# Sums of the resident weights made in DRAM by accumulating transfers instead of in pieces on GpSimd

## What is computed

```python
x = x + tanh(g_xattn[0]) * xattn(layernorm(x), ctx, mask, q_w, k_w, v_w, o_w, q_norm_w, k_norm_w)
x = x + tanh(g_ffn[0]) * ffn(layernorm(x), A, B, Wr)
# xattn: 16 batches of 128 rows, 32 query heads, 8 key/value heads of 128, RMS norm of q and k, softmax, output projection
# ffn: scores = x @ Wr.T, top 16 of 64 experts of rank 16, out = (x @ A * gates) @ B * 2
```

## Time and profile before

| | |
|---|---|
| median of three runs | 2540.8 us |
| the profiled execution | 2547.66 us, of it the span 2545.8 us |
| PE / DVE / ACT / POOL busy | 2323.6 / 1680.2 / 1178.5 / 1511.4 us |
| mean granted clock | 0.965 of full |
| moved by DMA | 427.69 MB, 168 GB/s |

### The profile page before, as it was taken

The page is one execution under the profiler, slowest core; times in us unless marked ns, Lnnn a source line. Parts: engine busy times, 40 slices in busy tenths (PEclk is TensorE's granted clock), DMA queues, the critical chain, the costliest instruction groups (busy, mean ns, idle before and its releaser), DMA issues.

```text
span 2545.8 us, 35745 instructions
## 1 busy us (share of the span) xinstructions
PE 2323.6 (91%) x11384; PEld 1929.5 (76%) x11384; DVE 1680.2 (66%) x2631; ACT 1178.5 (46%) x3731; POOL 1511.4 (59%) x2134
## 2 busy tenths in 40 slices
PE   5998996999999989999999799999998998878899
PEld 4886884888777778887888688788787876666687
DVE  6656556777677787766777835755757877454755
ACT  4545554556565676655666722322324234232321
POOL 6877557777677767766765344644655665334431
PEclk8999998999999999999999799999999998989899
DMA  4767565444444464444432544546455578564753
GB/s 175 252 200 256 157 219 170 121 133 132 130 133 129 120 224 133 133 133 133 133 104 86 182 160 152 198 156 211 162 166 199 182 215 273 148 227 128 242 174 140
DMA packets 329770, 427.69 MB, mean 168 GB/s; under 512 B 16240, under 2 KB 238704, under 8 KB 317552
## 3 DMA queue, kind: packets, MB, share of 16 engines
q1 hardware_dynamic: 329584, 425.39, 52.3%
HBM read 275.91 MB, written 149.42 MB: 167 GB/s over the span
## 4 chain that ended last, share of the span: by engine, by line
PE 41%; POOL 24%; DMA 20%; issue 7%; DVE 5%; SPq 2%; ACT 1%; POOLq 0%; ACTq 0%; DVEq 0%
PE bank L773 13%; PE bank L775 13%; PE bank L774 13%; DMA mini_combo<-in_sets 9%; DMA combos<-mini_combo 4%; POOL s_hi L1730 4%; POOL staged L1720 2%; POOL staged L1724 2%; POOL staged L1718 2%; DVE s_lo L1276 2%; POOL mini_combo L1808 2%; DMA gates_of_ranks<-gates_t 2%; POOL mini_combo L1805 1%; POOL mini_combo L1810 1%; POOL mini_combo L1806 1%
## 5 line engine op out<-in xcount | busy, mean ns | idle before, releaser
L773 PE MATMUL bank<-t_hi,s_hi 128*128 128x512 f32 x2720 | 1116.4, 410 | 120.6 <-DVE s_lo L1276 50.1
L775 PE MATMUL bank<-t_hi,s_lo 128*128 128x512 f32 x2720 | 1081.4, 398 | 0.0
L774 PE MATMUL bank<-t_lo,s_hi 128*128 128x512 f32 x2720 | 1080.0, 397 | 0.0
L1276 DVE TENSOR_TENSOR s_lo<-staged,s_hi 128x512 fp32r<-128x512 f32 x676 | 571.1, 888 | 211.8 <-ACT s_hi L1007 148.6
L773 PEld LDWEIGHTS bank<-t_hi,s_hi 128*128 128x128 f32 x2720 | 523.5, 192 | 236.8 <-issue 85.7
L775 PEld LDWEIGHTS bank<-t_hi,s_lo 128*128 128x128 f32 x2720 | 522.0, 192 | 116.2
L774 PEld LDWEIGHTS bank<-t_lo,s_hi 128*128 128x128 f32 x2720 | 524.7, 193 | 94.8
L1007 ACT CAST s_hi<-staged 128x512 fp32r<-128x512 f32 x452 | 260.5, 622 | 428.8 <-DMA staged<-heads 194.8
L1718 POOL TENSOR_TENSOR staged<-staged 128x512 f32<-128x512 f32 x96 | 136.4, 1421 | 305.7 <-DMA staged<-gated 104.3
L1386 DVE SCALAR_TENSOR_TENSOR probs<-bank,small,mask 128x128 f32<-128x128 f32 x512 | 144.0, 343 | 163.3 <-POOL small L1710 109.1
L1101 ACT ACTIVATE probs<-probs,small 128x128 f32<-128x128 f32 x512 | 198.0, 387 | 53.5 <-DVE small L1390 52.5
(11 more groups left out here) (124 smaller groups left out, 3225.8 us busy)
## 6 DMA issues: line engine op xcount, KB each, us to landing
heads<-heads SPq DMA_DIRECT2D x128, 256.0 KB, 3.7
t_raw<-combos SPq DMA_DIRECT2D x24, 1024.0 KB, 9.0
staged<-in_w_q SPq DMA_DIRECT2D x32, 768.0 KB, 5.7
staged<-heads SPq DMA_DIRECT2D x32, 768.0 KB, 5.9
t_raw<-in_sets SPq DMA_DIRECT2D x22, 1024.0 KB, 8.8
mini_combo<-in_sets SPq DMA_DIRECT2D x80, 256.0 KB, 3.4
combos<-mini_combo SPq DMA_DIRECT2D x80, 256.0 KB, 2.3
sums<-sums SPq DMA_DIRECT2D x18, 1024.0 KB, 7.9
```

What stands on the lines that cost most here:

```text
L773: nc.tensor.matmul(out[:, :], s_hi[w][:, cols], t_hi[k][:, at, :], start=start, stop=False, skip_group_check=True)
L774: nc.tensor.matmul(out[:, :], s_hi[w][:, cols], t_lo[k][:, at, :], start=False, stop=False, skip_group_check=True)
L775: done = nc.tensor.matmul(out[:, :], s_lo[w][:, cols], t_hi[k][:, at, :], start=False, stop=at == 3, skip_group_check=True)
L1276: return nc.vector.tensor_tensor(out, whole, hi.bitcast(FP32), ALU.subtract)
```

## The change

The tiles `combo` and `mini_combo` and all GpSimd arithmetic on them go, and with them all loads and stores of the pieces (84 loads, 84 stores). Each of the sets 1 to 6 gets four steps instead:

- step 0, SP: two transfers from DRAM to DRAM of 2 MB each copy blocks 0, 1, 0 and 2 of the set to `combos`;
- step 1, GpSimd issues a transfer that adds blocks 2 and 3 (2 MB, read from `sets`) to the sums 2 and 3 in DRAM;
- step 2, another adds sum 3 to sum 0 (1 MB); step 3, another adds sum 0 to sum 1 (1 MB).

For set 1 the steps are in entries 1 to 4, step 0 after `values_out` in beat 5, the others in beat 4. For sets 2 to 6 they are in rounds 2 to 5, 6 to 9, 10 to 13, then 14, 17, 18 and 19, and 20 to 23: step 0 at the end of slot 3 on SP, steps 1 to 3 in slot 2 on GpSimd behind `sums`. Every step waits for the whole of the one before. An accumulating transfer can only add, so the signs are turned: the sums of the moving operand are additions only, and in exchange some sums of the stationary operand, and some of the combinations of results, become differences (`minus`, `from_bank`), one operation for one of the same kind, engine, shape and place.

```diff
-    pc = m.put("combo", [P, 4, HALF])
+    m.put("b21_room", [P, 4, HALF])
...
-    mc = m.put("mini_combo", [P, 4, P])
...
-    def combo_unit(e):
-        return e - 1 if 1 <= e <= 4 else None
...
-    MINI_SLOTS = [(n, r) for n in range(32) if n not in (15, 31) for r in (0, 1, 3)][:80]
...
+    def combo_steps(e):
+        if 1 <= e <= 4:
+            return [(1, e - 1)]
+        return [(2 + u // 4, u % 4) for u, n in enumerate(n for n in range(2, 24) if n not in (15, 16)) if e == QA0 + n]
...
-                if k == 0 and which == 1:
-                    sp.wait_ge(pc_out, 64)
-                elif k == 0:
-                    sp.wait_ge(mc_out, 256 * (which - 1))
+                if k == 0:
+                    sp.wait_ge(combo_added, 48 * which)
...
-        def mini_in(u):
-            which, at = mini_piece(u)
-            if u:
-                sp.wait_ge(mc_out, 16 * u)
-            sp.dma_start(mc[:, :, :], d.sets[which, :, :, at].rearrange("b p c -> p b c")).then_inc(mc_in, 16)
...
+        def combo_copies(e):
+            for which, step in combo_steps(e):
+                if step == 0:
+                    if which > 1:
+                        sp.wait_ge(combo_added, 48 * (which - 1))
+                    sums, raw = d.combos[which].rearrange("b p c -> p b c"), d.sets[which].rearrange("b p c -> p b c")
+                    sp.dma_start(sums[:, 0:2, :], raw[:, 0:2, :]).then_inc(combo_copied, 16)
+                    sp.dma_start(sums[:, 2:4, :], raw[:, 0:4:2, :]).then_inc(combo_copied, 16)
...
+        def combos(e):
+            for which, step in combo_steps(e):
+                sums, raw = d.combos[which], d.sets[which]
+                if step == 0:
+                    continue
+                if step == 1:
+                    pool.wait_ge(combo_copied, 32 * which)
+                    to, part = sums[2:4].rearrange("b p c -> p b c"), raw[2:4].rearrange("b p c -> p b c")
+                if step == 2:
+                    pool.wait_ge(combo_added, 48 * which - 32)
+                    to, part = sums[0], sums[3]
+                if step == 3:
+                    pool.wait_ge(combo_added, 48 * which - 16)
+                    to, part = sums[1], sums[0]
+                nc.gpsimd.dma_start(to, part, accum_op=ALU.add, max_dma_last_dim=8192).then_inc(combo_added, 16)
...
-        def mini(u):
...
-            pool.wait_ge(mc_in, 16 * (u + 1))
-            nc.gpsimd.tensor_tensor(mc[:, 3, :], mc[:, 3, :], mc[:, 2, :], ALU.subtract).then_inc(mc_sum, 1)
-            nc.gpsimd.tensor_tensor(mc[:, 2, :], mc[:, 2, :], mc[:, 0, :], ALU.subtract).then_inc(mc_sum, 1)
...
         def third_product(e):
...
-            plus(ev[:, :], usum[:, :], 2)
+            from_bank(ev[:, :], 2, usum[:, :])
```

More of the change, by code:

```diff
@@ L671, in _ @@
                     values_out(e, 0)
-                    if combo_unit(e + 1) is not None and e < 15:
-                        combo_in(combo_unit(e + 1), pc)
+                    combo_copies(e)
                 if j == 6 and e and e % 2 == 0:
@@ L701, in _ @@
                     keys_out(15, 1)
-                if u is not None:
-                    mini_in(u)
-                if (n, r) == (30, 0):
-                    mini_out(79)
+                if r == 3:
+                    combo_copies(e)
         heads_out(127)
@@ L1826, in _ @@
         pool.wait_ge(t0_combo_pool, 1)
-        nc.gpsimd.tensor_tensor(t_raw[6][:, :, :], b21_again[:, :, :], t_raw[1][:, :, :], ALU.subtract).then_inc(t0_combo_pool, 1)
+        nc.gpsimd.tensor_tensor(t_raw[6][:, :, :], b21_again[:, :, :], t_raw[1][:, :, :], ALU.add).then_inc(t0_combo_pool, 1)
         for e in range(KV0, QA0):
             for j in SEVEN:
-                if j == 1 and combo_unit(e) is not None:
-                    combos(combo_unit(e), pc)
+                if j == 4:
+                    combos(e)
                 if j == 2 and e:
@@ L1862, in _ @@
                     values_high(n - 1)
-                if (n, r) in mini_at:
-                    mini(mini_at[n, r])
+                if r == 2:
+                    combos(e)
         for e in range(O0, A0):
```

79 lines of the change are left out of this document (21 added, 58 removed).

## The result

The changed kernel takes **2466.2 us** in the median of three executions (2465.9 to 2469.3), the kernel before 2540.8; the ratio is 0.9708, with a 95% interval of 0.9689 to 0.9727. A fourth execution took 3804.1 us at a granted clock of 0.557, and is left out here (with it the median would be 2467.8). The prediction was 2483, range 2456 to 2526.

The account below looks back on a forecast made before the run. TensorE, busy 91% of the span, was taken as near its bound, with pieces adding 3 us to a round's 29.31. Terms -77.6 + 7 + 5 + 3 + 5 = -57.6 us from the median 2540.8 gave 2483 us, range 2456 to 2526.

Parts of the forecast that it names:

- (a): Rounds 2 to 14: without pieces each falls to TensorE's own 29.31 us, a gain of 37.8 us.
- (b): Rounds 17 to 27: without pieces each falls to 29.31 us, a gain of 27.8 us.
- (d): Attention rounds, slot 2: 15 issues of adds on GpSimd cost 7 us (0 to 14).
- (e): Five rounds with copies: transfers behind them on SP's queue, such as `staged`, come late; 5 us in all (0 to 20).
- (c): The start, round 1 and just earlier: TensorE's waits of 15.1 us tied to pieces go, of which 12 us counted as gain.
- (f): Round 15: the copies of set 5 delay the refill issued 13.8 us later; cost 3 us (0 to 9).
- (g): Entry 1: the copies of set 1 delay the load of `staged` for entry 3; cost 5 us (0 to 11).
- (h): Accumulating transfers on GpSimd's queue: each has a round, 29.3 us, enough down to 72 GB/s; cost nothing.
- (i): The turned signs: as many operations of the same kinds, cost nothing.
- the pieces did not set the pace: Rival: late rounds are fast for other reasons, so steady rounds gain next to nothing; 2536 to 2550 us, chance 0.06.
- slower by the adds: Rival: accumulating transfers miss their round and GpSimd waits in slot 2; 2598 us at 40 GB/s, chance 0.07.
- The traffic rival: Rival: the gain comes, but issues and copies cost their upper ends, with copies near 23 us; 2510 to 2535 us, chance 0.19.

Follow-up runs that it names:

- No arithmetic: Kernel before with all loads, stores and waits of pieces kept, but one sum of four columns per piece instead of four of 128; 2466.6 us.
- no loads: Kernel before with only the first piece loaded, its four sums and the store still made for all 80 pieces; 2464.4 us.
- the copies ahead of `staged`: Changed kernel with the copies of sets 2 to 6 put on SyncE's queue just ahead of the next load of `staged`, not two slots behind it; 2501.7 us.
- the first experiment: Kernel before with its 80 pieces starting two rounds later, in rounds 2 to 14 and 16 to 29; 2518.3 us.
- no adds: Changed kernel without the three adds of set 1, its copies kept; 2456.8 us.
- small adds: Changed kernel with set 1's three adds in place, as many rows, but only 16 columns (64 bytes) each instead of 2048 (8 KB); 2459.1 us.
- odd entries: Changed kernel with set 1's copies in entry 0 and its adds in entries 1, 3 and 5; 2461.1 us, ratio to the kernel before 0.9697.

## Why the prediction came out as it did

The sum was -57.6 us and the traces show -81.8; the difference of 24.2 is made of 10.6 in (a), (b), (d) and (e) together (-53.6 predicted, -64.2 found in those rounds), 10.2 in (c), 4.0 in (f), -2.2 in (g), and 1.5 in the rest of the program.

The total lies in the range and 17 us below the forecast; most of the errors point the same way, so it isn't luck of terms that cancel.

**(a) and (b), the steady rounds: right in size, half right in cause.** 37.8 and 27.8 were predicted, 37.0 and 27.2 came, and the three rounds without pieces were a true measure of TensorE's bound. But the text put the 3 us down to GpSimd's wait for loads. No arithmetic, which left 45.5 of the 96.4 us of waits, ran as fast as no pieces, and so did no loads. By the rule above the wait cost because sums stood beside it and the two together went past GpSimd's room of some 10 us. The price was safe, since it was read from the rounds as wholes, and not from the cause.

**(c), the start: too small, 12 against 22.2.** The term took TensorE's two waits, 15.1 us, took 12 of them, and left out what follows a wait. Rounds 0 and 1 again, now for all engines (busy time of PE, PEld, DVE, ACT and POOL, granted clock, DMA share, GB/s), kernel before and changed kernel:

```profile
399.66:428.46 28.80, 25.12 (x100) 20.91 (x101) 17.11 (x14) 10.05 (x19) 23.10 (x22) 0.81 0.34 101
428.46:473.98 45.52, 31.77 (x157) 26.53 (x157) 24.97 (x47) 16.77 (x79) 29.85 (x59) 0.85 0.44 128
```
```profile
407.29:429.64 22.35, 22.32 (x100) 18.45 (x100) 20.18 (x16) 10.05 (x20) 21.95 (x16) 0.90 0.27 78
429.64:459.38 29.74, 28.41 (x157) 23.82 (x156) 22.11 (x44) 16.77 (x78) 20.86 (x40) 1.00 0.42 129
```

TensorE idles 17.4 of 74.3 us before and 1.4 of 52.1 after: 16.1 us are pauses that are gone. For the same 257 matmuls it is busy 56.9 us before and 50.7 after: 6.2 us are clock. The step that failed is "of which I take 12": the stop was priced 4 us too low, the slow stretch behind it not at all. In the kernel before the granted clock is 0.50 from 444 to 448 us, behind 8 us without a matmul, and 1.00 from 452 to 468, with TensorE busy nearly all through. The Trainium skill, TensorE: Matmul & The Clock Gate, Part 1, says that the clock follows how busy the array has lately been; these rows, at 1.2 and at 2.4 GHz, agree.

**(d) and (e), issues and copies: too large, 12 against 1.4.** An issue takes 1.24 or 0.88 us, about the upper bound of 0.9, but the place has room for it: 0.27 us of a first add reach the round, where I had counted 0.45 of each issue. The copies of a set, 4.2 MB, land 13.9 us behind the first issue (13.2, and 0.66 between the two), which is 300 GB/s read and as much written. C = 13.9 lies below the 20.5 from which `staged` would be late, so the term is nothing by the prediction's own formula. The reasoning of that step is what the copies ahead of `staged` confirm: late by 7.3 us as soon as the distance is gone. What was too cautious was the value between two far bounds. With the 20 us that the Trainium skill, DMA: Bandwidth & Descriptors, section Latency and other measured facts, suggests for such copies, the sum would have been worse, 2490; the page's figures are for rows at a pitch of 512 KiB or more, which these copies don't have, and the measured 13.9 decides.

**(f), rounds 15 and 16: the other sign, 3 lost against 1.0 gained.** The copies go out 14 us ahead of the refill and take 13.9, so nothing is left in its way.

**(g), set 1: the mechanism right, the size short, 5 against 7.2.** The prediction named the load of `staged` for entry 3 behind the copies, and that load lands after 9.7 us in place of 4.5. By the prediction's own formula, late by C - 12, the measured C makes 1.9 us; the copies alone cost 2.9 over entries 2 to 4. What it missed is the first add, which (d) had waved through, "in idle time of GpSimd": with `staged` late there is no idle time left at that place, so the issue delays GpSimd's sums further, and the 2 MB delay the `staged` of the entry after. That the total came near 5 is in part luck, the more so as the 7.2 are those of one pair of traces. The five traces with the entries 0 to 15 of the kernel before take 375.4 to 380.6 us for them, the four with those of the changed kernel 387.8 to 392.1, and the means differ by 11.5. "Their removal brings nothing" did hold: the gain in these entries is none.

**(h) and (i): nothing, as predicted.** An add of 2 MB lands in 13.8 us, 152 GB/s, where 72 sufficed and 51 was the point at which the sign would turn. With the turned signs VectorE has as many instructions as before.

Of the rivals, "the pieces did not set the pace" falls with the first experiment, "slower by the adds" with the adds' 13.8 and 8.3 us, even in short rows. The traffic rival's condition, C near 23, isn't met; but its mechanism is real, and costs 34 us once the copies are put in the wrong place.

What stays open is how the 3.4 us of the issue part between GpSimd's delay and VectorE's; no run separates these.

## What to carry to other kernels

Count a background job on an in-order engine, waits and work together, against the time for which that engine idles when the job is gone; in the steady rounds here it was free below some 10 us, and above that nearly each microsecond counted. When it moves into DMA, its cost is set by its place on the queue: put large transfers, copies or adds, right behind a load that is soon needed, never less than their landing time ahead of the next one. Where a wait of TensorE goes or comes, price the granted clock behind it too.

## What the runs showed of the hardware

- **Copies within DRAM** ran at 4.2 MB in 13.9 us, 300 GB/s in each direction, where loads moved 366 GB/s. I had set the bounds at 11.5 and 23 us.
- **An accumulating transfer** from DRAM to DRAM landed 2 MB after 13.8 us and 1 MB after 8.3. Two plain copies side by side landed twice the 2 MB in the same 13.9 us, so a byte took the add twice as long; a plain copy of 2 MB alone was not measured. Rows of 1 KB instead of 8 made it 9.7 us.
- **Issuing one from GpSimd** took 1.24 us for 256 rows of 8 KB, 0.88 for 128, and 1.34 for 1024 rows of 1 KB, so a row more costs about 0.5 ns. The 256 rows lie in two blocks and cost 0.3 us more than that; that the second block is the reason isn't shown.
- **VectorE is slow beside GpSimd's sums.** Two halves of `s_lo` that usually take 1.29 us together took 4.30 us in entry 3 of the changed kernel, beside an issue and two sums on GpSimd. The kernel before has a case in entry 5 beside the same two sums with no issue:

```profile
141.25 2.96 DVE L1276 TENSOR_TENSOR s_lo<-staged,s_hi 128x512 fp32r<-128x512 f32 x2 [1.69 <-ACT s_hi L1007]
```

  Beside three sums of `combo` it took 3.45 us (at 59.18). The Trainium skill, SBUF — State Buffer, section Who interferes with whom, says that an addition on VectorE with both inputs in SBUF contends with GpSimd's reads; the 2.96 and 3.45 us agree with that. Whether the issue adds to it, or only moved GpSimd's two sums so that both fell wholly on the two halves, no run separates.
- **A short pause and the clock.** In entry 3, a pause of TensorE of 2.8 us left the granted clock at 1.00 (no adds), and one of 3.7 us was followed by a mean of 0.87 over the entry (small adds); over entries 2 to 4 the second run lost 0.9 us more in pauses and 2.5 us in slower matmuls. After pauses of 3.8 us in the changed kernel and 3.3 in odd entries the means were 0.94 and 0.93.
